# Attention input of a transformer block: modulated and split token-major on GpSimd, transposed by DMA instead of on TensorE

## The reference

```
mod = silu(c) @ wmod -> sa, ca, ga, sb, cb, gb          # (8, 512) each, ga and gb kept at least 0.25 in size
h = layernorm(x) * (1 + ca) + sa
q, k, v = (h @ W + b).reshape(b, 16, 32, 1024)           # 16 heads of 32, t = 1024
attn = softmax(einsum('bhdt,bhds->bhts', k, v) * temperature)
x = x + ga * einsum('bhdt,bhts->bhds', q, attn)
h = layernorm(x) * (1 + cb) + sb
scores = h @ w_router; the 512 tokens with the highest go through gelu(h @ W1 + b1) @ W2 + b2,
    weighted with sigmoid(score) and added to h
x = x + gb * (that)
```

## Time and profile before

| | |
|---|---|
| median of three runs | 2307.62 us |
| the profiled execution | 2308.37 us |
| its span | 2306.6 us, TensorE clock granted 0.994 |
| TensorE busy | 2249.3 us (98%) |
| VectorE busy | 1901.7 us (82%) |
| ScalarE busy | 1485.1 us (64%) |
| GpSimd busy | 1244.2 us (54%) |

### The profile page before, as it was taken

How to read it: one execution, slowest core, us unless ns; L and a number is a source line. 1 busy time by engine, 2 the same in 40 slices (tenths; PEclk the granted TensorE clock), 3 DMA queues, 4 the chain that set the end, 5 groups by cost and what they waited for, 6 DMA issues and landing times.

```text
span 2306.6 us, 35648 instructions
## 1 busy us (share of the span) xinstructions
PE 2249.3 (98%) x12746; PEld 879.7 (38%) x12746; DVE 1901.7 (82%) x2912; ACT 1485.1 (64%) x2621; POOL 1244.2 (54%) x1114
## 2 busy tenths in 40 slices
PE   7999999999999999999999999997989999999998
PEld 3333333333333333333333333331434444444443
DVE  6999999999999999999999999998863563563543
ACT  3888888888888888888888888888211111111110
POOL 5667766676666777666776667761542312302300
PEclk9999999999999999999999999999999999999999
DMA  7333343333333333333333333343331111201200
GB/s 242 85 78 79 77 107 74 79 92 73 83 97 74 74 78 94 86 71 90 78 75 91 83 74 85 77 86 105 116 87 51 53 35 51 67 21 51 60 19 19
DMA packets 121266, 179.81 MB, mean 78 GB/s; under 512 B 43736, under 2 KB 43736, under 8 KB 120576
## 3 DMA queue, kind: packets, MB, share of 16 engines
q1 hardware_dynamic: 111152, 152.03, 26.9%
q0 software_dynamic: 9728, 25.23, 3.6%
q10 hardware_dynamic: 208, 0.28, 0.1%
HBM read 67.18 MB, written 43.16 MB: 48 GB/s over the span
## 4 chain that ended last, share of the span: by engine, by line
PE 77%; DVE 13%; POOL 3%; ACT 3%; issue 2%; DMA 1%; SPq 0%; ACTq 0%; POOLq 0%; DVEq 0%
PE acc L641 17%; PE sc L592 17%; PE sc L795 13%; PE sc L782 12%; PE pj L604 10%; DVE nmax L1079 8%; PE pj L616 6%; ACT probs L863 2%; PE sc L627 1%; POOL x L1427 1%; DVE qn L1131 1%; DVE stats L1113 1%; ACT room L841 1%; DMA out<-base 1%; POOL hbuf L1436 0%
## 5 line engine op out<-in xcount | busy, mean ns | idle before, releaser
L863 ACT ACTIVATE probs<-sc,nmax 128x1024 f32<-128x1024 f32 x1024 | 1138.6, 1117 | 205.8 <-DVE nmax L1079 195.4
L1079 DVE TENSOR_REDUCE nmax<-sc 128x1 f32<-128x1024 f32 x1024 | 1214.6, 1214 | 41.5 <-PE sc L592 38.5
L641 PE MATMUL acc<-probs,qn 128*32 128x512 f32 x4096 | 545.8, 605 | 3.4 <-DVE x L1108 1.9
L958 ACT ACTIVATE probs<-sc,b_col 128x512 f32<-128x512 f32 x128 | 87.9, 687 | 485.0 <-PE sc L782 436.7
L604 PE MATMUL pj<-room 128*128 128x512 f16 x1500 | 385.2, 379 | 2.6 <-POOL room L1413 2.4
L795 PE MATMUL sc<-room,probs 128*128 128x512 f16 x1536 | 354.6, 381 | 8.4 <-DVE hbuf L1274 7.8
L592 PE MATMUL sc<-room 128*128 128x512 f16 x1024 | 308.2, 383 | 11.8 <-DMA room<-room 5.7
L592 PE MATMUL sc<-stacks 128*128 128x512 f16 x1024 | 308.4, 383 | 9.2 <-ACT probs L863 8.9
L1290 DVE CAST probs<-probs 128x512 f16<-128x512 f32 x128 | 62.6, 489 | 247.9 <-ACT probs L958 202.1
L795 PEld LDWEIGHTS sc<-room,probs 128*128 128x128 f16 x1536 | 150.7, 98 | 191.7 <-DVE probs L1292 8.3
L604 PEld LDWEIGHTS pj<-room 128*128 128x128 f16 x1500 | 146.1, 98 | 182.1 <-ACT room L834 7.6
(11 more groups left out here) (166 smaller groups left out, 2233.8 us busy)
## 6 DMA issues: line engine op xcount, KB each, us to landing
stacks<-room SPq DMA_DIRECT2D x512, 64.0 KB, 2.0
room<-room SPq DMA_DIRECT2D x508, 64.0 KB, 2.0
h_rows<-hbuf SPq DMA_DIRECT2D x132, 128.0 KB
out<-base SPq DMA_DIRECT2D x132, 128.0 KB
room<-in_L_attn_x SPq DMA_DIRECT2D x96, 128.0 KB, 2.8
rows<-mod_rows SPq DMA_DIRECT2D x32, 256.0 KB, 4.3
room<-in_L_ffn_W SPq DMA_DIRECT2D x8, 1024.0 KB, 5.2
probs<-in_L_wmod SPq DMA_DIRECT2D x4, 1024.0 KB, 13.5
```

The costliest lines, as they stand in the source:

```text
L641: mm = nc.tensor.matmul(acc[at:at + DH, :], qn[:, (p // 2) % 2, p % 2, h2, :], probs[:, (2 * p + h2) % PROBS, half * D:(half + 1) * D], st ...
L863: nc.scalar.activation(probs[:, u % PROBS, :], slot(g, ring_at(p, h2)), ACT.Exp, bias=nmax[:, u % PROBS:u % PROBS + 1], accum_out=rsum[:, ...
L958: nc.scalar.activation(g32[:, f % 2, :], ff[f % 2], ACT.Gelu_apprx_tanh, bias=b1_col[:, f:f + 1], scale=1.0 / WS).then_inc(gelu_done, 1)
L1079: nc.vector.tensor_reduce(nmax[:, u % PROBS:u % PROBS + 1], slot(g, ring_at(p, h2)), AX.X, ALU.max, negate=True).then_inc(max_done, 1)
```

## The change

GpSimd now applies the modulation itself, with tokens on partitions: it multiplies `xhat` by the broadcast row 1 + ca behind pair 0 (`times_scale`), adds the row sa behind pair 2 (`plus_shift`) and splits into fp16 halves `x16` behind the residual of pair 4 (`split_x`). SyncE transposes the halves by eight DMAs per group into `hT16`: four for the high half right after the loads of x, four for the low half between the replication of the keys and that of the values. TensorE's transposes, the evacuation by ScalarE, `split_hT` in the loop and the 33rd ring entry go. The broadcast rows come from DRAM (`first_rows`, written once at the start), two loads per batch. The first two groups are still prepared on TensorE. The order of partitions within a tile changes from (h2, t) to (t, h2) throughout, with as many instructions.

```diff
+            sp.wait_ge(s_scale, 1)
+            for i in range(4):
+                sp.dma_start(first_rows[:, i // 2, (i % 2) * (D // 2):(i % 2 + 1) * (D // 2)], first_sb[DH * i:DH * i + B]).then_inc(s_fst, 16)
             for cc in range(CC):
                 sp.dma_start(wb_stage[cc], w_mod[cc * P:(cc + 1) * P, 2 * D:6 * D]).then_inc(s_wb[cc], 16)
...
+            def load_first_rows(b):
+                for j in range(2):
+                    sp.dma_start(mod_x[:, j, :], first_rows[b, j].partition_broadcast(P)).then_inc(s_mx, 16)
+
+            sp.wait_ge(s_fst, 4 * 16)
+            load_first_rows(0)
+
+            def transpose_x(n, a):
+
+                if a == 0:
+                    sp.wait_ge(q_pe, 2 * (n - 1))
+                sp.wait_ge((s_hi, s_ht)[a], n + 1)
+                columns = hT16[n % 2][:, a].rearrange("q c (t s e) -> q t s c e", t=2, s=SUBS)
+                for s in range(SUBS):
+                    for t in range(2):
+                        at = 2 * DH * t
+                        sp.dma_start_transpose(columns[:, t, s], x16[at:at + 2 * DH, a, s, :]).then_inc(s_xt, 16)
...
                     if not (last and g >= GB - 3):
                         load_x((g + 3) % 4, ahead[g])
+                    if not (last and g >= GB - 2):
+                        transpose_x(b * GB + g + 2, 0)
+                    if g == 1 and not last:
+                        sp.wait_ge(s_xm, 2 * (b * GB + g + 1))
+                        load_first_rows(b + 1)
...
                         replicate((g + 1) % 2, 0, b * GB * 4 + 4 * (g + 1) + 2)
...
+                        if not (last and g >= GB - 2):
+                            transpose_x(b * GB + g + 2, 1)
                         replicate((g + 1) % 2, 1, b * GB * 4 + 4 * (g + 1) + 4)
...
-                                    pe.wait_ge(s_ht, b * GB + g + 2)
+                                    pe.wait_ge(s_ht, 2)
+                                    if b or g:
+                                        pe.wait_ge(s_xt, prepared(b * GB + g + 1))
...
-                        if 2 * p + 2 == T_AT and not (last and g >= GB - 2):
-                            pe.wait_ge(s_xhat, b * GB + g + 3)
-                            pe.wait_ge(slot_free, freed(b, g, T_AT))
-                            transposes(slot(g, T_AT))
...
+            def times_scale(n):
+
+                b = n // GB
+                pool.wait_ge(s_xhat, n + 1)
+                pool.wait_ge(s_mx, 32 * (b + 1))
+                nc.gpsimd.tensor_tensor(xhat, xhat, mod_x[:, 1:2, :].broadcast_to([P, SUBS, D]), ALU.mult).then_inc(s_xm, 1)
+                pool.wait_ge(s_xm, 2 * (n - 1) - 1)
+
+            def plus_shift(n):
+
+                nc.gpsimd.tensor_tensor(xhat, xhat, mod_x[:, 0:1, :].broadcast_to([P, SUBS, D]), ALU.add).then_inc(s_xm, 1)
+                pool.wait_ge(s_xm, 2 * (n - 1))
+
+            def split_x(n):
+
+                if n > 2:
+                    pool.wait_ge(s_xt, prepared(n - 1))
+                nc.gpsimd.tensor_scalar(x16[:, 0], xhat, 1.0, 1.0, ALU.mult, ALU.mult).then_inc(s_hi, 1)
+                pool.wait_ge(s_hi, n + 1)
+                nc.gpsimd.tensor_tensor(x16[:, 1], xhat, x16[:, 0], ALU.subtract).then_inc(s_ht, 1)
...
                         normed_x((g + 2) % 4, n3)
+                        times_scale(n3 - 1)
...
+                    if prep:
+                        plus_shift(n3 - 1)
...
                     residual(b, g)
+                    if prep:
+                        split_x(n3 - 1)
...
-                    if prep:
-                        split_hT(g % 2, n3, (slot_free, freed(b, g, T_AT) + SLOTS))
                     base_times(b, g)
```

More of the change, by code:

```diff
@@ L129, in store_kept, with block_phases @@
                                      bounds_check=B * KEEP - 1, oob_is_err=False).then_inc(r.s_sel, 16)
-def block_phases(nc, x, w_qkv, b_qkv, temperature, w_router, w_ffn, c, w_mod, out, h_rows, mod_rows, sel_rows, score_rows, r):
+def block_phases(nc, x, w_qkv, b_qkv, temperature, w_router, w_ffn, c, w_mod, out, h_rows, mod_rows, first_rows, sel_rows, score_rows, r):
     scores = r.scores
@@ L310, in block_phases @@
         s_one = sem("s_one")
-        s_table = sem("s_table")
+        s_scale = sem("s_scale")
+        s_fst = sem("s_fst")
+        s_mx = sem("s_mx")
+        s_xm = sem("s_xm")
+        s_xt = sem("s_xt")
         s_now = sem("s_now")
@@ L358, in block_phases @@
         UNITS = 2 * PAIRS
[L359 to L360 removed]
+        RING = UNITS
         LAG = 4
         def ring_at(p, h2):
[L365 to L366 removed]
+            return 2 * p + h2
         def freed(b, g, v):
@@ L378, in pair_no, with slot, prepared @@
             return b * (GB * PAIRS) + (g * PAIRS + p + 1)
-        def slot(g, v):
-            return sc[:, (g * RING + v) % SLOTS, :]
-        assert GB * RING % SLOTS == 0 and GB * UNITS % PROBS == 0
+        def slot(b, g, v):
+            return sc[:, ((b * GB + g) * RING + v) % SLOTS, :]
+        def prepared(n):
+            return 16 * 4 * SUBS * (n - 1)
+        assert GB * UNITS % PROBS == 0
         ALL_PAIRS = NG * PAIRS + LAG
@@ L591, in scores_of @@
                 for half in range(2):
-                    mm = nc.tensor.matmul(slot(g, v)[:, half * D:(half + 1) * D],
+                    mm = nc.tensor.matmul(slot(b, g, v)[:, half * D:(half + 1) * D],
                                           stacks[g % 2][:, 0, hq, i * P:(i + 1) * P],
@@ L639, in products @@
                     for half in range(2):
-                        at = DH * (2 * h2 + half)
+                        at = DH * (2 * half + h2)
                         mm = nc.tensor.matmul(acc[at:at + DH, :], qn[:, (p // 2) % 2, p % 2, h2, :],
@@ L930, in body @@
                             kept_high(0, KEPT_AT.index(p - 1), aux[0])
-                        no_entry = last and g >= GB - 2
-                        exp_unit(b, g, p, 1, 2 if no_entry and 2 * p + 2 == T_AT else 1)
-                        if 2 * p + 2 == T_AT and not no_entry:
-                            if g == 2:
-                                nc.scalar.activation(mod_now[:], mod_table[:, b + 1, :], ACT.Identity).then_inc(s_now, 1)
-                                act.wait_ge(s_now, b + 2)
-                            act.wait_ge(s_ht, b * GB + g + 2)
-                            evac_t(slot(g, T_AT), b * GB + g + 3).then_inc(slot_free, 1)
+                        exp_unit(b, g, p, 1)
             for b in range(B - 1):
@@ L1018, in _ @@
             last.then_inc(s_now, 1)
-            for m, add in ((1, 1.0), (0, 0.0)):
-                part = slice((1 - m) * CC, (2 - m) * CC)
-                after = mod_table[:, B, part].rearrange("p (h k) -> p h k", h=2)
-                nc.vector.tensor_scalar(after, cols[:, m, :, :, B - 1], add, None, ALU.add)
-                for h in range(2):
-                    table = mod_table[:, 0:B, (1 - m) * CC + 2 * h:(1 - m) * CC + 2 * h + 2].rearrange("p b k -> p k b")
-                    last = nc.vector.tensor_scalar(table, cols[:, m, h, :, 0:B], add, None, ALU.add)
-            last.then_inc(s_table, 1)
+            nc.vector.tensor_scalar(first_sb[2 * DH:4 * DH], first_sb[2 * DH:4 * DH], 1.0, None, ALU.add).then_inc(s_scale, 1)
             def split_w(k, w16):
@@ L1354, in _ @@
             for j in range(P // DH):
-                h2, t = j // 2, j % 2
+                t, h2 = j // 2, j % 2
                 rows_j = slice(DH * j, DH * (j + 1))
                 nc.gpsimd.iota(r.tok_i[rows_j], pattern=[[P, B * TB]], base=2 * DH * h2 + t, channel_multiplier=2)
-                part = r.earlier[rows_j].rearrange("q (h t d) -> q h t d", h=2, t=2)
+                part = r.earlier[rows_j].rearrange("q (t h d) -> q t h d", h=2, t=2)
                 last = nc.gpsimd.affine_select(out=part, in_=part, compare_op=ALU.is_gt, fill=0.0, base=2 * DH * h2 + t,
-                                               pattern=[[-2 * DH, 2], [-1, 2], [-2, DH]], channel_multiplier=2)
+                                               pattern=[[-1, 2], [-2 * DH, 2], [-2, DH]], channel_multiplier=2)
             last.then_inc(r.s_const, 1)
@@ L1495, in body @@
                     if prep:
-                        pool.wait_ge(t_pe, b * GB + g + 2)
+                        if n3 == 3:
+                            pool.wait_ge(t_pe, 2)
+                        else:
+                            pool.wait_ge(s_ht, n3 - 1)
                         normed_x((g + 2) % 4, n3)
+                        times_scale(n3 - 1)
                     if last and g == GB - 2:
```

30 lines of the change are left out of this document (14 added, 16 removed).

## The result

The changed kernel takes 2333.86 us (median of 4 runs, 2333.31 to 2339.45) against 2307.24 us before (2303.21 to 2310.8): ratio 1.0121, 95% interval 1.0107 to 1.0136. 26.6 us slower; the forecast said 26.7 and 2335 us. The profiled execution took 2333.66 us with a span of 2331.9. (The 2307.62 us given ahead of the prediction was the median of three of these four runs of the kernel before.)

A forecast was written before the change was run, and what follows sets the result against it. The prediction took VectorE to set the pace of the attention stage. Its terms, 28.8 - 4.7 + 2.6 = 26.7 us on 2308.4, gave 2335 us, range 2318 to 2350 (chance 0.55).

The forecast's parts named there:

- The lock at pairs 2 and 4: VectorE's qn multiplies there wait for GpSimd's two-input passes to end: 0.96 us a group, 28.8 us for 30.
- near 1.0: Expected sign in the new profile: the qn multiply of pair 10 lasts near 1.0 us, longer than 0.46.
- VectorE sets the pace, so whatever makes it late is paid in full: Attention stage: VectorE, busy 386 of 400 us, is the bound, so any delay to it counts fully.
- The transposes' removal gains 0: Dropping TensorE's transposes gains 0, since GpSimd's work fixes the end of the qn multiply at pair 10.
- the other case: VectorE's two waits for scores around TensorE's transposes are gained after all: at most 0.52 us a group, 15.6 us.
- split_hT leaves the gap behind pair 12: GpSimd no longer runs over there, so the qn multiply of pair 14 falls to 0.29 us: 4.7 us gained.
- SyncE: Eight transposing DMAs per group fit in its queue at T, the issue time, of 0.6 to 1.2 us: cost 0.
- the threshold of 1.5: SyncE's queue: nothing is late while one transposing issue takes up to 1.5 us.
- The start: Kernel start: 0.52 MB of broadcast rows queue ahead of the first replication, costing 2.6 us.
- rival 1: Slow transposing DMAs make SyncE the bound from 1.5 us an issue; 2455 us at 1.99; chance 0.20, 2350 to 2600.
- The passes fit: New GpSimd passes end before the qn multiplies, making the kernel faster: 2288 us, or near 2291; chance 0.14.
- No change: Delays at pairs 2 and 4 are made good in VectorE's remaining waits: 2301 to 2315 us; chance 0.11.

The follow-up runs named there:

- experiment 1: Changed kernel with the normalization moved behind pair 14 of the group before and both new row passes behind pair 0: 2313.04 us, ratio 1.0038 to the kernel before.
- experiments 3: Kernel before with h_times moved behind pair 10, h_plus behind pair 12, split_hT behind h_plus and base_times behind pair 14: 2310.57 us, ratio 1.0014.
- experiment 8: Kernel before with the fourth split's low half computed for 8 of 512 columns: 2304.49 us; the same with the moves of experiments 3 added: 2354.51 us.
- fit1: The same run as experiment 1: 2313.04 us.
- fit4_plain: Changed kernel with GpSimd's passes placed so every qn multiply takes 0.29 us, row loads issued earlier, and plain DMAs replacing transposing ones (input not transposed): 2266.55 us.
- experiment 4: Changed kernel with each transposing DMA replaced by a plain one of 64 KB, leaving the transposition out: 2326.09 us, ratio 1.0085 to the kernel before.
- fit5: fit4_plain with real transposing DMAs, the high half split behind pair 2 and its four transposes issued before SyncE waits for the residual: 2280.63 us.
- before_free: Kernel before with the moves of experiments 3 and the fourth split's low half computed for 8 of 512 columns: 2354.51 us, ratio 1.0207.
- before_low: Kernel before with the fourth split's low half moved behind pair 12 and the last row multiplication behind pair 14: 2356.24 us, ratio 1.0223.

## Why the prediction was right

The number is right to 1 us, and the new term that it named, the lock, is real. The account of the kernel before was wrong, one cost was missing, and several errors made each other good: the closeness is luck.

*The lock at pairs 2 and 4* (28.8 us, the term that decided): right in mechanism and size. Mean qn 0.76 and 0.75 us where 0.29 was, 0.93 together against 0.96, and experiment 1 takes out 0.93 in a clean group. In the group of the earlier trace rows pair 10 stands 1.16 us ("near 1.0"), the period is 49.43 ("about 49.3"), and there is no wait for scores behind pair 9. The lock is also what the Trainium skill says ("SBUF — State Buffer", section "Who interferes with whom": a VectorE instruction with two SBUF inputs contends with a GpSimd instruction that reads SBUF, and the ports that they share are an exclusive lock); the multiplies ending 0.14 us behind the GpSimd operation agree, and so does the multiply held by a one-input operation in experiment 1.

*"VectorE sets the pace, so whatever makes it late is paid in full"*: false for the kernel before. There TensorE waited 1.7 us in 1400, its chain fills a clean group, and the locks of pairs 10 and 12 cost nothing when taken out (experiments 3 and 8). The prediction had the chain, 77% TensorE, and set it aside on the ground that TensorE shows as busy even while it waits; the changed kernel shows such waits, at 387 of 400 us busy. A VectorE that is busy 386 of 400 us had its locked time counted as work, and was about 0.46 us a group short of being the bound (48.40 against the 47.94 of fit1). So of the 0.93 us of new locks the clean group pays 0.47.

*"The transposes' removal gains 0"*: right from pair 6 to pair 10 of the group shown, 12.60 against 12.61 us, and for the reason given. For the group as a whole it is what takes TensorE's share from 48.4 down to 47.2 us and leaves VectorE as the bound. The bound given for the other case, 15.6 us, was too small: 1.2 us a group, 36 us over 30, are to be had once the locks are gone (fit4_plain reaches them), and they are TensorE's transposes and what stands around them, as the sum in experiment 8 shows.

*split_hT leaves the gap behind pair 12* (4.7 us gained): the multiply fell from 0.45 to 0.29 in the mean, as said. In the kernel before it stood where TensorE was the bound, so that it was worth 4.7 us there is not shown; not tested alone.

*SyncE* (hidden, cost 0, T 0.6 to 1.2 us): T is 1.25, just above, and the threshold of 1.5 was worked out for one quiet group. Group 0 has 6.2 us more, and experiment 4 shows 13.6 in the attention stage, 7.8 in the total. This is the mis-sized term. The estimate from the Trainium skill's "VectorE: DVE Perf Modes" had T at 2.6 us, twice too high, and the total at about 2600. That transposing DMAs are as fast as regular ones ("Advanced Engine Details and Errata" of the Trainium skill, "X-Bar Transpose (TRN2)") holds nearly for the landing, 2.4 us against 2.1, and not for the issue, 1.25 against 0.60, and in this kernel the issue is what the queue had no room for.

*The start* (2.6 us): the first scores of the kernel start at 47.20 in place of 43.93, 3.3 later. In seven variants of the changed kernel they begin between 44.19 and 46.84, so this term varies from profile to profile.

*What makes the sum come out.* In the two profiled executions: start +3.3, attention +31.3, feed-forward -9.3, together +25.3. The attention stage was to cost 24.1 (28.8 - 4.7). It cost less by the half of the locks that TensorE had room for, and more by SyncE's 13.6. The feed-forward stage was to cost 0. Its -9.3 is mostly one wait of VectorE for a store:

```profile
DVE gb_b L1282 <- DMA out<-base: 2.7, 1, 2.7
```

It was 9.4 us before and 4.2 to 8.2 in eleven other profiles, so these two executions hold its extremes. The total is closer than its terms are.

*The range.* Its lower end is called half of the lock term; half of 28.8 below 2335 is 2321, not 2318.

*The rivals.* The slow DMA is present: 13.6 us of attention where the estimate of rival 1 gave some 270. "The passes fit" is false as written, and true once they are placed so: that is fit1. "No change" fell, though a part of it is right: half of each new lock was made good, by the room that TensorE's pace left to VectorE and not by VectorE's waits for scores.

*Open:* what the 14 us are that fit5 still loses to fit4_plain, and what each of the three things around the transposes (TensorE's own 1.07 us, the ring entry, ScalarE's evacuation) is worth by itself.

## What to carry to other kernels

Before giving an idle engine a new pass, lay it on the timeline of the engine it shares ports with: idle share says nothing, what matters is whether one of its operations runs into a two-input operation of the other, and whether that other engine is the bound. A lock costs its full length where the locked engine sets the pace and nothing where another does. A busy share does not say which it is, since a locked instruction counts as busy: add up what each engine has to do in one period, compare the sum with the period, and look which engine's matmuls or reductions never wait. And count a new DMA by the time that its issue takes in its queue, along the whole chain that follows it: speeding up the rest makes the same queue late.

## What was not expected

- A transposing DMA of 64 KB (64 partitions x 512 fp16) holds SyncE's queue 1.25 us, a plain one between the same buffers 0.60, though they land in 2.4 and 2.1 us.
- TensorE was the bound of the kernel before, at 48.4 us a group, with VectorE half a microsecond behind it. The change took 1.2 us off TensorE and put 0.93 us of locks on VectorE, and so moved the bound.
- The lock reaches 2.07 us: the router product went from 0.68 to 2.75 us when a GpSimd operation of 2.37 us started 0.17 us ahead of it. One such collision per group goes with before_free and before_low being 49 and 50 us slower.
- Eight extra issues of 0.48 us each cost 145 us over 30 groups, 4.8 us per group for 3.86 us of queue, at a granted clock of 0.97 in place of 1.00.
